# Bias rows in a four-layer decoder kernel: one bf16 product of three rows that opens a group, in place of an f32 product of one row per block of 128 tokens

## The reference

```
x = _layernorm(x + _L0_attn_ref(x, L0_attn_W_attn, L0_attn_W_k2, L0_attn_W_proj), axis=-1)
x = _layernorm(x + _L0_xattn_ref(ctx_1024, x, L0_xattn_gamma_x, L0_xattn_beta_x, L0_xattn_gamma_l, L0_xattn_beta_l, L0_xattn_Wq, L0_xattn_Wkv, L0_xattn_Wo), axis=-1)
...
```

```
value = (x @ W_value + b_value).reshape(Bq, T, heads, hd).transpose(0, 2, 1, 3)
off = (x @ W_off + b_off).reshape(Bq, T, heads, P, 2)
...
return attn @ W_out + b_out
```

## Time and profile before

| | us |
|---|---|
| median of 3 runs | 3131.95 |
| lowest and highest run | 3117.47 and 3134.06 |
| span of the profiled execution (first to last instruction) | 3111.5 |
| PE busy | 2550.3 |
| DVE busy | 1773.7 |
| ACT busy | 1298.5 |
| POOL busy | 679.2 |

### The profile page before, as it was taken

One profiled execution on the slowest core, in us unless ns is written; L12 is line 12 of the kernel. 1 busy time (PEld: TensorE's weight loads), 2 busy tenths in 40 slices (PEclk: granted clock), 3 DMA queues, 4 the chain that ended last, 5 costly groups with the idle time before them and its releaser, 6 DMA issues.

```text
span 3111.5 us, 38689 instructions
## 1 busy us (share of the span) xinstructions
PE 2550.3 (82%) x13120; PEld 1322.1 (42%) x13201; DVE 1773.7 (57%) x4879; ACT 1298.5 (42%) x3060; POOL 679.2 (22%) x917
## 2 busy tenths in 40 slices
PE   4788897799987887878658988977999888878865
PEld 2333335334543585234323333443345446743343
DVE  5544437635564597744566534485256547887164
ACT  1555621443324442563425555215432344335741
POOL 1420002411101484100123100014201126830000
PEclk7899898879887998999869999997798789989986
DMA  5100002200000002200121000022001000021000
GB/s 179 30 1 1 1 1 53 54 2 21 24 24 0 1 1 55 56 1 31 29 56 18 1 1 1 1 53 55 1 21 35 14 1 1 28 55 29 1 1 7
DMA packets 43591, 73.35 MB, mean 24 GB/s; under 512 B 4417, under 2 KB 36225, under 8 KB 41602
## 3 DMA queue, kind: packets, MB, share of 16 engines
q1 hardware_dynamic: 42818, 69.59, 9.4%
q10 hardware_dynamic: 576, 1.29, 0.1%
HBM read 43.86 MB, written 1.05 MB: 14 GB/s over the span
## 4 chain that ended last, share of the span: by engine, by line
PE 58%; DVE 20%; ACT 9%; issue 7%; POOL 2%; DMA 1%; SPq 1%; another core or an unknown queue 0%; ACTq 0%; DVEq 0%; POOLq 0%
PE psum L565 4%; PE psum L994 4%; PE psum L555 3%; DVE floor_s L2266 3%; PE psum L2167 3%; PE psum L1005 3%; ACT PT_s L1026 3%; DVE mx_s L707 2%; PE psum L1542 2%; PE psum L1359 2%; PE psum L1372 2%; PE psum L743 2%; PE psum L818 2%; PE psum L1834 2%; PE psum L972 2%
## 5 line engine op out<-in xcount | busy, mean ns | idle before, releaser
L634 ACT ACTIVATE PT_s<-psum 128x512 f32<-128x512 f32 (+3 forms) x768 | 343.0, 498 | 249.3 <-PE psum L555 233.8
L386 POOL TENSOR_SCALAR ve<-mv 128x4 f32<-128x4 f32 x48 | 13.4, 279 | 1563.4 <-DVE mv L376 1563.2
L538 PE MATMUL psum<-KS_s,QS_s 128*128 128x512 bf16 (+3 forms) x730 | 227.5, 364 | 108.0 <-DMA KS_s<-parts_s 43.8
L2193 POOL TENSOR_TENSOR buffer<-sim_s 128x1024 f32<-128x1024 f32 x128 | 270.7, 2130 | 156.6 <-DVE floor_s L2266 87.0
L704 DVE CUSTOM_DVE_ANT_0 rest_s<-psum,packed_early 128x128 f32<-128x128 f32 (+3 forms) x512 | 224.3, 487 | 58.3 <-PE psum L538 56.6
L555 PE MATMUL psum<-QS_s,KS_s 128*128 128x512 bf16 (+3 forms) x725 | 223.4, 354 | 32.0 <-ACT PT_s L634 15.5
L565 PE MATMUL psum<-PT_s,vaug 128*9 128x512 f32 (+3 forms) x1536 | 174.3, 528 | 67.6 <-POOL PT_s L677 53.4
L677 POOL TENSOR_SCALAR_AFFINE_SELECT PT_s<-PT_s 128x128 f32<-128x128 f32 x512 | 147.3, 298 | 358.8 <-ACT PT_s L634 354.0
L2226 ACT ACTIVATE above_s<-buffer,below_s 128x1024 f32<-128x1024 f32 x128 | 145.4, 1149 | 129.5 <-PE psum L2167 80.0
L1044 ACT ACTIVATE PT_s<-psum 128x512 f32<-128x512 f32 (+1 forms) x224 | 121.1, 592 | 162.8 <-PE psum L996 162.8
L2167 PE MATMUL psum<-packed_early,above_s 128*128 128x128 f32 x1024 | 142.9, 285 | 50.5 <-DVE floor_s L2266 44.4
(11 more groups left out here) (449 smaller groups left out, 5069.3 us busy)
## 6 DMA issues: line engine op xcount, KB each, us to landing
buffer<-packed_experts SPq DMA_DIRECT2D x36, 384.0 KB, 3.5
QS_s<-parts_s SPq DMA_DIRECT2D x96, 128.0 KB
KS_s<-parts_s SPq DMA_DIRECT2D x192, 64.0 KB
buffer<-packed_moe SPq DMA_DIRECT2D x4, 2048.0 KB, 8.1
buffer<-packed_cross SPq DMA_DIRECT2D x4, 2048.0 KB, 7.6
buffer<-packed_product SPq DMA_DIRECT2D x4, 1024.0 KB, 5.0
packed_early<-packed_early SPq DMA_DIRECT2D x1, 2654.0 KB
raw_s<-packed_setup SPq DMA_DIRECT2D x1, 1840.0 KB, 7.0
```

Source lines behind the costliest of these rows:

```text
L538: pe.matmul(bank[n % 4][:, 0:n_keys], QS[:, h // 2, j * P:(j + 1) * P], KS[:, h % 2, h // 2, 0:n_keys], start=True, stop=True).then_inc(ri ...
L634: a.activation(PT[:, u // 4 % 2, i, q0_of(c):T], bank[u % 3][:, q0_of(c):T], ACT.Exp, scale=scale).then_inc(exp_done.sem, 1)
L2193: g.tensor_tensor(fs[:, n % 2], m[:, 0, :].unsqueeze(2).to_broadcast([P, NK, NK]), m[:, 1, :].unsqueeze(1).to_broadcast([P, NK, NK]), ALU. ...
```

## The change

A three-row copy of all bias rows is made in setup: POOL splits the packed f32 row into a bf16 row, the bf16 row of what is left, and the bf16 row of what is left after that (five operations on one partition, in series), and SP loads the three rows from one partition onto three (`rows3`). `packed_row` is loaded second on SP now, with a semaphore of its own, and SP waits for the new load at the end of setup. `ones3` is a bf16 tile of 3 by 128 ones.

At every place above one product now opens the group: `ones3` is stationary, the three bf16 rows are the moving operand, and it writes the columns of all four blocks at once with the same rows (an access pattern with step 0 over the blocks): 512 columns for the 128-column biases, 256 for the logits, 32 for the router, 128 for the values of 77 and 14 rows. The value products follow with `start=False`. The bias product stands behind the same wait as the value products did, with one exception: in the last projection of `l2_attn` it is issued before the wait, right behind L2005.

```diff
+def add_rows(pe, s, out, rows, m=P):
+    return pe.matmul(out, s.ones3[:, 0:m], rows, start=True, stop=False, skip_group_check=True)
...
+def over_blocks(rows):
+    return rows.unsqueeze(1).to_broadcast([3, TJ, rows.shape[1]])
...
@@ attention8
+            if bv is not None:
+                add_rows(pe, s, blocks(bank[2]), over_blocks(bv))
             for c in range(KC):
-                o = bank[2][:, c * P:(c + 1) * P]
-                mm = pe.matmul(o, s.xT[:, c * P:(c + 1) * P], wv, start=True, stop=bv is None)
-                if bv is not None:
-                    mm = pe.matmul(o, s.ones[0:1, :], bv, start=False, stop=True)
+                mm = pe.matmul(bank[2][:, c * P:(c + 1) * P], s.xT[:, c * P:(c + 1) * P], wv, start=bv is None, stop=True, skip_group_check=True)
...
@@ project_out
+        if bo is not None:
+            add_rows(pe, s, blocks(s.bank[3]), over_blocks(bo))
         for j in range(TJ):
...
-            if bo is not None:
-                mm = pe.matmul(o, s.ones[0:1, :], bo, start=False, stop=True)
...
@@ the router
-            pe.matmul(o, s.xT[:, j * P:(j + 1) * P], s.w["wrT"][:], start=True, stop=False)
-            mm = pe.matmul(o, s.ones[0:1, :], s.w["rb"][:], start=False, stop=True)
+        add_rows(pe, s, blocks(bank[3], 8), over_blocks(s.w3["rb"]))
+        for j in range(TJ):
+            mm = pe.matmul(bank[3][:, j * 8:(j + 1) * 8], s.xT[:, j * P:(j + 1) * P], s.w["wrT"][:], start=False, stop=True, skip_group_check=True)
...
@@ l2_attn, start
+        add_rows(pe, s, blocks(bank[0]), over_blocks(s.w3["boff"]))
+        add_rows(pe, s, blocks(bank[1], HP), over_blocks(s.w3["batt"]))
+        add_rows(pe, s, bank[2][0:R, 0:D], s.w3["bval"], R)
...
@@ l2_attn, end
         pe.matmul(bank[0], s.w["wout"][:], mT[:], start=True, stop=True).then_inc(out_ready.sem, 1)
+        add_rows(pe, s, blocks(bank[3]), over_blocks(s.w3["bproj"]))
         yield end + 6
         pe.wait_ge(*out_copied(1))
...
@@ setup, SP
             sp.dma_start(raw[:], t["setup"]).then_inc(raw_loaded, 16)
+            sp.dma_start(k.row[:], t["row"]).then_inc(row_loaded, 16)
             for dst, src in loads:
                 sp.dma_start(dst, src).then_inc(loaded, 16)
+            sp.wait_ge(row_split, 5)
+            sp.dma_start(k.rows3[:], row_parts[:]).then_inc(row_spread, 16)
+            sp.wait_ge(row_spread, 16)
...
@@ setup, POOL
+            g.wait_ge(row_loaded, 16)
+            g.tensor_copy(row_parts[:, 0, :], k.row[:]).then_inc(row_split, 1)
+            g.wait_ge(row_split, 1)
+            g.tensor_tensor(row_left[:], k.row[:], row_parts[:, 0, :], ALU.subtract).then_inc(row_split, 1)
...
+            g.tensor_copy(row_parts[:, 2, :], row_left[:]).then_inc(row_split, 1)
             g.wait_ge(floored, 1)
             g.tensor_tensor(inv_sim[:], inv_sim[:], k.minus_half[:], ALU.pow).then_inc(inverted, 1)
```

More of the change, by code:

```diff
@@ L1346, in tensor @@
         pe.matmul(bank[0][:], wq, s.xT[:], start=True, stop=True).then_inc(projected.sem, 1)
-        pe.matmul(bank[2][0:nk, 0:P], s.ctxT[:], wv, start=True, stop=False)
-        pe.matmul(bank[2][0:nk, 0:P], s.ones[0:1, 0:nk], bv, start=False, stop=True).then_inc(projected.sem, 1)
+        add_rows(pe, s, bank[2][0:nk, 0:P], bv, nk)
+        pe.matmul(bank[2][0:nk, 0:P], s.ctxT[:], wv, start=False, stop=True, skip_group_check=True).then_inc(projected.sem, 1)
         yield T1
@@ L2463, in program @@
             k.w.update(views(packed[group], places[group]))
-        loads = [(packed["early"][:], t["early"]), (packed["row"][:], t["row"])]
+        k.row = packed["row"]
+        k.rows3 = sb("rows3", [3, t["row"].shape[1]], BF16)
+        k.w3 = views(k.rows3, {name: (at, (3,) + shape[1:]) for name, (at, shape) in places["row"].items()})
+        loads = [(packed["early"][:], t["early"])]
         for name, arr in t["constants"].items():
@@ L2471, in program @@
         late_loaded = ctx.enter_context(nc.semaphore("late_loaded"))
-        setup_sems = [ctx.enter_context(nc.semaphore(f"setup{i}")) for i in range(13)]
+        setup_sems = [ctx.enter_context(nc.semaphore(f"setup{i}")) for i in range(16)]
         streams = []
@@ L2575, in setup @@
     squares = s0.tile("ones_square", [P, P])
-    raw_loaded, loaded, ready, squared, summed, floored, inverted, sig, weff_ready, chain, quantised, turned, copied = sems
+    n_row = t["row"].shape[1]
+    row_left = s0.tile("row_left", [1, n_row])
+    row_parts = s0.tile("row_parts", [1, 3, n_row], BF16)
+    row_loaded, row_split, row_spread, raw_loaded, loaded, ready, squared, summed, floored, inverted, sig, weff_ready, chain, quantised, turned, copied = sems
     turns = []
@@ L2638, in _ @@
             v.memset(k.ones[:], 1.0)
+            v.memset(k.ones3[:], 1.0)
             for s in streams:
```

38 lines of the change are left out of this document (21 added, 17 removed).

## The result

The changed kernel takes 3033.35 us (median of 4 runs, 3028.01 to 3035.73), the kernel before 3133.01 us (4 runs). The ratio is 0.9699, with a 95% interval of 0.9672 to 0.9725: 3.0% faster. The forecast was 3072, a gain of 60 us; the gain is 94 us by the ratio. Neither is in the 3045 to 3095 of the forecast itself: both lie where the prediction had rival 2, with a chance of 0.11. The same kernel was measured twice more beside other experiments, at 0.9728 (0.9702 to 0.9755) and 0.9740 (0.9723 to 0.9757). All ratios leave out slow runs; there was one, of 4667.68 us, among the ten of experiment 1.

What follows compares the result with a forecast made beforehand. The prediction took PE to bound the kernel most of the time. PE's 66 + 22 + 3 - 14 = 77 us, times 0.8, less 2 for setup, gave 60 us: 3131.95 to about 3072; forecast 3045 to 3095, range 3035 to 3110.

Steps and rivals of the forecast that it cites:

- rival 2: Whole span: PE's saving passes on whole and fewer low-clock stretches are met; 3046, or 3036 with the clock; chance 0.11.
- What is removed: Bias products between value products: their 76.9 us of busy time go wholly, 66 us of PE's time.
- What gets faster beside it: Value products beside bias products: 0.222 us each instead of 0.416, saving 22 us (15 to 25); layer-3 projections 3 us.
- What is added: The new three-row bf16 opening products: 0.31 us for a wide one, 0.2 for a narrow one, 14 us (8 to 25).
- PE's sum: PE's time over all places: 66 + 22 + 3 - 14 = 77 us less, bounds 59 and 86.
- Setup: Start of the kernel: the row split on POOL and the three rows' load cost 2 us, bounds 0 and 5.
- How much reaches the end: Both streams' coupling through the fixed order: a share of 0.8 of PE's saving arrives, 77 x 0.8 - 2 = 60 us.
- The clock: PE at output projections: granted clock 1.00 at one, 0.50 at another; busy sums hold both, so no factor is added.
- rival 4: Whole span: PE is busy for less time, the clock falls, slower than before; 0.01 off the clock adds 18 us; chance 0.04.
- The value lines: Sign in the profile after: six lines of value products show about half their busy time of before.
- The run of four: Sign in the profile after: four value products in a run take 0.89 us at the high clock.
- The wait of DVE: Sign in the profile after: DVE's wait for the output projection falls from 51.8 to about 30 us.

Runs made afterwards that it cites:

- experiment 1: The kernel before with only the changed setup: the three rows are made and loaded, but no product reads them; ratio 1.0028 to the kernel before.
- experiment 2: The kernel before with the changed setup and three-row bf16 bias products, still one behind each value product in the old order; ratio 0.9871 to the kernel before.
- experiment 4: The kernel before, old setup and order, each bias product replaced by an f32 one with operands of 128 rows, biases left out; ratio 0.9757 to the kernel before.
- experiment 6: The changed kernel with eight bf16 products of 128 rows and 512 columns ahead of each of 24 wide opening products; ratio 0.9862 to the kernel before.
- experiment 3: The changed kernel, each group opening with a run of four f32 one-row bias products instead of one bf16 product; ratio 0.9817 to the kernel before.

## Why the prediction came out as it did

- **What is removed** (66 us without the 14-row products): right. From start to start the bias products had 70 us, of which the 14-row ones 2.
- **What gets faster beside it** (22 us, and 3 in the layer-3 projections): right. The starts give 20 and 2 us, and experiments 2 and 4 show that the cause is the one named.
- **What is added** (14 us): right, 13 us by the starts; the narrow ones took 0.11 to 0.20 us at the high clock. For the wide one there was luck: the two products of the earlier trace rows start within 0.01 us of each other and run side by side, so the 0.31 us of the pair is no sum of two, as the prediction's bounds had it, and a single product of three rows takes 0.32.
- **PE's sum** (77 us): 80 us by the starts, 83 by busy time.
- **Setup** (2 us, bounds 0 and 5): too small. It was 5.6 us at the end of setup, 2.2 us for a time and 5.4 again ahead of the first place, and setup alone measured 3 to 15 us, with a lower clock. The mechanism was not the one worked out. POOL was done in time for its old operation; what was late was DVE, some of whose operations POOL's work on one partition had slowed while it ran.
- **How much reaches the end** (0.8): this is the step that failed, together with the clock below. With the 80 us of the starts, 85.2 us and what setup cost on top arrived in the profiled executions, a share of 1.1, of which some 5 us is work outside the places that ran at a higher clock; in the medians it is much the same (81 to 94). The prediction let the other stream's half be lost where that stream waits for DVE or ACT. But nothing was lost: PE's busy time fell by 82.8 us and its idle time did not grow. That both streams stood behind PE at the places, so that both gained, is the likely reason; it is argued from the earlier trace rows, and no run tests it by itself. Experiment 6 measures the share with products that leave the clock alone: 50.6 us of span for 46 us by the profiles, 42 by the medians, so 0.9 to 1.1.
- **The clock** was priced in rival 4 with the wrong sign. The prediction took a fall for possible because PE would be busy for less time. What counts here is what the products are made of and how they stand: the products of one row and of 128 in turn were followed by stretches at 1.2 GHz, and with them gone the mean clock rose by 0.012 and the low-clock time fell by 93 us (87 and 88 over all runs of the repeats). The same fall came with one-row products in a run (experiment 3) and with 128 rows in the old order (experiment 4), less than half of it with three rows in the old order (experiment 2). A higher clock was listed in rival 2 as a gain of 10 us; the result lies there. That the measured time is still about at the lower end of the stated range is owed to the range's width, which took part of that rival in, and not to the 60 us of the sum. The Trainium skill, "TensorE: Matmul & The Clock Gate", describes in its section on HAM oscillation how pauses of PE bring the clock down; here the clock was low from 710.71 on, behind 3.33 us without a pause, and with the same pauses in front of the places the changed kernel kept it at 1.00.

Of the signs that the prediction named, PE's busy time (2467.5, within 2460 to 2480) came out. The value lines did not: about half their busy time was expected, and it fell from 63.1 to 44.5 us (with the four runs without a bias taken out of L530, as before), 29%; from start to start they fell by the 20 us that were expected, since a record in a run is longer than the distance to the next. The run of four took 0.99 us and not 0.89. The wait of DVE is 36.3 us and not 30. And the mean clock moved by more than 0.01, which the prediction had named as a sign that its forecast is wrong and rival 2 is right.

## What to carry to other kernels

A product with one or a few rows costs more than its columns when it stands between products of 128 rows: each change cost 0.2 us in f32 here, and behind many of them in turn PE ran at half clock more often. Put such products together at the head of a group, or pad them to 128 rows with zeros, which costs no columns and was 17 us better by itself; 3 us of that are in the starts, and the rest came with a higher clock. And where two streams share an engine's fixed order and PE is what both queue behind, expect the time saved to arrive in full, as it did here (a share of 0.9 to 1.1 in experiment 6); what a stretch gives in which the other stream waits for something else, no run here measured.

## What the runs showed of the hardware

- PE with operands of 128 rows throughout took 0.22 us for an f32 product of 128 columns; in turn with products of one or three rows, 0.42 for the one of 128 rows. The few-row product itself had 0.41 in f32 and 0.15 in bf16. In runs of their own, four f32 products of one row took 1.08 us.
- 48 us of added products of three rows came with 80 us of span and 73 us more low-clock time, and 46 us of added products of 128 rows with 50.6 us of span and 23 us more, on the same columns and at the same places. But 44 products of three rows had no more low-clock time over all runs than none (671 and 680 us), and padded to 128 rows they had less (627).
- POOL's work on one partition slowed some of DVE's operations: 0.20 to 1.87 us and 1.32 to 3.70 us for two, and not at all the reduction (1.32) and the reciprocal (0.59); with the split on DVE and POOL idle the two were back at 0.20 and 1.32. A cast of 1240 columns on one partition took 0.79 us on DVE and 1.21 on POOL.
